# A hybrid layer kernel: the expert tiles' down product in three passes, one tile later

## The reference

```
x = x + mamba2(norm(x))        # 128 heads of 64, 8 groups, state 128
x = x + ffn(norm(x))
x = x + masked_linear(norm(x)) # 512 x 512, 32 x 32 blocks masked
x = x + ffn(norm(x))           # the same weights again
```

```
gu_s = x2 @ shared_w_gate_up.T ; g_s, u_s = split(gu_s)
shared_out = silu(g_s) * u_s @ shared_w_down.T
probs = softmax(x2 @ gate_w.T)
topk_vals, topk_idx = top_k(probs, 2)      # of 16 experts
topk_vals = topk_vals / sum(topk_vals)
g, u = split(einsum('th,eih->eti', x2, w_gate_up))   # 128 + 128 per expert
out_e = einsum('eti,ehi->eth', silu(g) * u, w_down)  # 128 -> 512
ffn = einsum('eth,te->th', out_e, combine) + shared_out
```

## Time and profile before

| what | us |
|---|---|
| median of 3 runs | 2001.85 |
| the profiled execution's own time | 1995.66 |
| its span, first to last instruction | 1993.9 |
| TensorE busy | 1960.6 |
| first tile loop, from the first tile's products | about 1656 to 1753.5 |
| second tile loop | about 1859 to 1957 |

### The profile page before, as it was taken

The page is one execution under the profiler, slowest core; times in us unless marked ns, Lnnn a source line. Parts: engine busy times, 40 slices in busy tenths (PEclk is TensorE's granted clock), DMA queues, the critical chain, the costliest instruction groups (busy, mean ns, idle before and its releaser), DMA issues.

```text
span 1993.9 us, 38125 instructions
## 1 busy us (share of the span) xinstructions
PE 1960.6 (98%) x11776; PEld 1632.7 (82%) x11776; DVE 1467.4 (74%) x2764; ACT 1191.9 (60%) x2602; POOL 1032.7 (52%) x907
## 2 busy tenths in 40 slices
PE   5999999999999999999999999999999999999999
PEld 4888888888888888888888888888888878877887
DVE  8998499849975997599759966996698673167315
ACT  4795388538853884388448744974496444534442
POOL 1596059616951694179417932792289315440433
PEclk8999999999999999999999999999999999999999
DMA  3552145114511351234123413341243139951996
GB/s 107 168 168 58 42 121 168 57 40 124 163 53 57 120 155 48 73 111 152 44 88 109 140 44 93 113 131 43 92 130 113 54 107 327 378 156 48 313 386 198
DMA packets 143909, 253.92 MB, mean 127 GB/s; under 512 B 21448, under 2 KB 37832, under 8 KB 143696
## 3 DMA queue, kind: packets, MB, share of 16 engines
q1 hardware_dynamic: 134848, 231.35, 36.8%
q0 software_dynamic: 7520, 16.80, 2.8%
q10 hardware_dynamic: 1328, 3.15, 0.4%
HBM read 233.38 MB, written 25.69 MB: 130 GB/s over the span
## 4 chain that ended last, share of the span: by engine, by line
PE 91%; DVE 5%; issue 2%; ACT 1%; DMA 1%; DVEq 0%; ACTq 0%; SPq 0%; POOL 0%; POOLq 0%
PE bank L1683 61%; PE bank L1802 7%; PE bank L1992 6%; PE bank L1816 6%; PE bank L1756 4%; PE bank L2004 3%; PE bank L1784 2%; DVE Y L1283 1%; PE bank L1979 1%; PE bank L1691 1%; DVE spare L1380 1%; PE bank L1775 1%; PE bank L1823 1%; DVE Y L1292 1%; DMA cv<-xn_dram,toks 0%
## 5 line engine op out<-in xcount | busy, mean ns | idle before, releaser
L1683 PE MATMUL bank<-xh,wh 128*128 128x512 f32 x1288 | 523.9, 407 | 7.4 <-POOL wl L720 4.0
L1683 PE MATMUL bank<-xh,wl 128*128 128x512 f32 x1288 | 504.9, 392 | 0.0
L1683 PE MATMUL bank<-xl,wh 128*128 128x512 f32 x1288 | 502.8, 390 | 0.0
L720 POOL TENSOR_TENSOR wl<-raw,wh 128x512 fp32r<-128x512 f32 x144 | 192.8, 1344 | 456.7 <-ACT wh L870 456.7
L1283 DVE SCALAR_TENSOR_TENSOR Y<-bank,cpar,Y 128x511 f32<-128x511 f32 (+2 forms) x384 | 286.8, 747 | 23.3 <-ACT Y L914 13.9
L1683 PEld LDWEIGHTS bank<-xh,wh 128*128 128x128 f32 x1288 | 243.0, 189 | 57.2 <-POOL wl L720 4.9
L1683 PEld LDWEIGHTS bank<-xh,wl 128*128 128x128 f32 x1288 | 242.3, 188 | 54.4
L1683 PEld LDWEIGHTS bank<-xl,wh 128*128 128x128 f32 x1288 | 243.4, 189 | 45.8 <-issue 0.5
L737 POOL TENSOR_TENSOR Y<-Y,gt 128x512 f32<-128x512 f32 x128 | 184.1, 1439 | 94.5 <-DVE gt L1337 92.7
L1345 DVE TENSOR_TENSOR al<-Y,ah 128x512 fp32r<-128x512 f32 x128 | 95.8, 749 | 184.3 <-ACT ah L972 184.3
L1683 PE MATMUL bank<-wh,ah 128*128 128x512 f32 x544 | 213.6, 393 | 0.5
(11 more groups left out here) (231 smaller groups left out, 4028.2 us busy)
## 6 DMA issues: line engine op xcount, KB each, us to landing
mem<-c_rows SPq DMA_DIRECT2D x128, 256.0 KB, 3.9
mem<-wffn_d SPq DMA_DIRECT2D x62, 512.0 KB, 6.2
E<-e_rows SPq DMA_DIRECT2D x256, 96.0 KB, 3.5
raw<-wconv_d SPq DMA_DIRECT2D x80, 256.0 KB, 3.0
cv<-c_rows SPq DMA_DIRECT2D x64, 256.0 KB, 4.0
spare<-c_rows SPq DMA_DIRECT2D x64, 256.0 KB, 4.1
raw<-wgate_d SPq DMA_DIRECT2D x64, 256.0 KB, 2.7
raw<-wout_d SPq DMA_DIRECT2D x64, 256.0 KB, 2.7
```

Of the source, the lines that this page charges most:

```text
L720: inc(pool.tensor_tensor(wl[:, W_SLOT[p], :], raw[:, R_SLOT[p], :], wh[:, W_SLOT[p], :], ALU.subtract), w_lo)
L1683: got = mm(out, l, r, start=first and n == 0, stop=last and n == 2)
```

## The change

The hidden rows and the expert's down weights are each split into a high and a low part, and the down product becomes three passes. ACT makes both high parts (`t_hid_hi`, `t_down_hi`), VectorE both low parts. They lie in free places of `ah`, `al`, `wh` and `wl`, two buffers for the weights and four for the hidden rows. TensorE's down product moves from iteration k+1 of a tile to k+2, and with it the output and the store; the loops of TensorE, ACT and SP have one iteration more. The buffers of the down weights and of the hidden rows are released by VectorE's subtraction (`td_lo`, `th_lo`) and no longer by TensorE's product (`ty_mm`). The first high part of the second shared half's hidden rows waits for all down products, since it uses the same memory. The four semaphores `fraw_in` are merged with `raw_in`.

```diff
@@ SP
             def tile_down(run, tau):
                 if tau >= DN_RING:
-                    sp.wait_ge(ty_mm, job(run, tau - DN_RING) + 1)
+                    sp.wait_ge(td_lo, job(run, tau - DN_RING) + 1)
                 elif run:
-                    sp.wait_ge(ty_mm, TILES)
+                    sp.wait_ge(td_lo, TILES)
...
-                for k in range(TILES + 1):
+                for k in range(TILES + 2):
...
-                    if k:
-                        tile_out(run, k - 1)
+                    if k >= 2:
+                        tile_out(run, k - 2)
@@ ACT
+                if i % 2:
+                    act.wait_ge(ty_mm, job(i // 2, TILES))
...
                 if tau >= H_RING:
-                    act.wait_ge(ty_mm, job(run, tau - H_RING) + 1)
+                    act.wait_ge(th_lo, job(run, tau - H_RING) + 1)
...
+            def t_down_hi(run, tau):
+                act.wait_ge(td_in[tau % DN_RING], 16 * uses(DN_RING, run, tau))
+                if tau < 2:
+                    now(act, dn_mm, 2 * run, TT)
+                else:
+                    act.wait_ge(ty_mm, job(run, tau - 2) + 1)
+                nc.scalar.activation(down_rows(tau, 0), tdn[tau % DN_RING], ACT.Copy).then_inc(td_hi, 1)
+
+            def t_hid_hi(run, tau):
+                act.wait_ge(tg_h, job(run, tau) + 1)
+                if tau >= 4:
+                    act.wait_ge(ty_mm, job(run, tau - 4) + 1)
+                nc.scalar.activation(hid_rows(tau, 0), thid[tau % H_RING], ACT.Copy).then_inc(th_hi, 1)
...
                     if 0 <= k < TILES:
                         t_tanh(run, k)
+                        t_hid_hi(run, k)
                     if k + 2 < TILES:
                         t_rows_evac(run, k + 2)
-                    if 0 <= k - 1:
-                        t_out(run, k - 1)
+                    if 0 <= k - 1 < TILES:
+                        t_down_hi(run, k - 1)
+                    if 0 <= k - 2:
+                        t_out(run, k - 2)
@@ VectorE, at the end of t_hidden, and behind it
+                    dve.wait_ge(th_hi, n)
+                    TTn(hid_rows(tau, 1), hid, hid_rows(tau, 0), ALU.subtract).then_inc(th_lo, 1)
+
+                def t_down_lo(tau):
+                    dve.wait_ge(td_hi, job(run, tau) + 1)
+                    TTn(down_rows(tau, 1), tdn[tau % DN_RING], down_rows(tau, 0), ALU.subtract).then_inc(td_lo, 1)
...
                 for tau in range(TILES):
                     t_hidden(tau)
+                    if tau:
+                        t_down_lo(tau - 1)
+                    if tau == TILES - 1:
+                        t_down_lo(tau)
@@ TensorE
                 def t_down(tau):
-                    pe.wait_ge(tg_h, job(run, tau) + 1)
-                    pe.wait_ge(td_in[tau % DN_RING], 16 * uses(DN_RING, run, tau))
+                    pe.wait_ge(th_lo, job(run, tau) + 1)
+                    pe.wait_ge(td_lo, job(run, tau) + 1)
...
-                    mm(bank[YB[tau % 2]][:, :], thid[tau % H_RING], tdn[tau % DN_RING], start=True,
-                       stop=True).then_inc(ty_mm, 1)
+                    three(bank[YB[tau % 2]][:, :], hid_rows(tau, 0), hid_rows(tau, 1), down_rows(tau, 0),
+                          down_rows(tau, 1), True, True, True).then_inc(ty_mm, 1)
...
-                for k in range(TILES + 1):
+                for k in range(TILES + 2):
...
-                    if k:
-                        t_down(k - 1)
+                    if k >= 2:
+                        t_down(k - 2)
```

More of the change, by code:

```diff
@@ L287, in hybrid_layer @@
         dn_acc = counted("dn_acc", TT)
-        fraw_in = [sem(f"fraw_in{n}") for n in range(NRAW)]
         sp_in, spm_in, rt_in = sem("sp_in"), sem("spm_in"), sem("rt_in")
@@ L306, in hybrid_layer @@
         tx_mm, tx_ok = sem("tx_mm"), sem("tx_ok")
+        td_hi, td_lo, th_hi, th_lo = sem("td_hi"), sem("td_lo"), sem("th_hi"), sem("th_lo")
         tg_mm, tg_th, tg_hg, tg_h = sem("tg_mm"), sem("tg_th"), sem("tg_hg"), sem("tg_h")
@@ L468, in hidden_rows, with down_rows, hid_rows @@
             return (wl if low else wh)[:, s, :].rearrange("p (a b) -> p a b", a=4)
+        def down_rows(tau, low):
+            return (al if low else ah)[:, tau % 2, :, :].rearrange("p a b -> p (a b)")
+        def hid_rows(tau, low):
+            return (wl if low else wh)[:, 10, tau % 4 * P:(tau % 4 + 1) * P]
         def job(run, tau):
@@ L563, in shared_in @@
                 sp.dma_start(raw[:, p % NRAW, :], wffn_d[3 * (EXPERTS + 2 * (i % 2)) + p]).then_inc(
-                    fraw_in[p % NRAW], 16)
+                    raw_in[p % NRAW], 16)
             experts = wffn_d[0:3 * EXPERTS].rearrange("(e k) p n -> e p k n", k=3)
@@ L630, in fraw_arrived @@
         def fraw_arrived(eng, i, p):
-            eng.wait_ge(fraw_in[p % NRAW], 16 * (i * (2 if p % NRAW < 2 else 1) + (2 if p >= NRAW else 1)))
+            mixer = GROUPS * R_COUNT[p % NRAW]
+            eng.wait_ge(raw_in[p % NRAW], 16 * (mixer + i * (2 if p % NRAW < 2 else 1) + (2 if p >= NRAW else 1)))
         @block.gpsimd
@@ L1119, in _ @@
                 hidden_hi(first, 3)
-                for k in range(-2, TILES + 1):
+                for k in range(-2, TILES + 2):
                     if 0 <= k < TILES:
                         t_tanh(run, k)
+                        t_hid_hi(run, k)
                     if k + 2 < TILES:
                         t_rows_evac(run, k + 2)
-                    if 0 <= k - 1:
-                        t_out(run, k - 1)
+                    if 0 <= k - 1 < TILES:
+                        t_down_hi(run, k - 1)
+                    if 0 <= k - 2:
+                        t_out(run, k - 2)
                     if 1 <= k <= 4:
```

## The result

The change made the kernel slower: 2013.79 us, median of 5 runs (2011.96 to 2017.07), against 2003.16 (2001.73 to 2006.36) for the kernel before on the same chip. The ratio, in brackets its 95% interval, is 1.0058 [1.0046, 1.007], 11.6 us of loss (the two medians differ by 10.6) where I had forecast 3.2 of gain. 2013.79 lies above my range, which ended at 2008.5.

The account below looks back on a forecast made before the run. TensorE, busy 98% of the span, was taken as the bound, with DMA nearly full beside it. Beats near 3.05 us made 93.95 us per run, 3.2 us gained in all: 1998.7 us forecast, range 1992 to 2008.5.

Parts of the forecast that it names:

- VectorE's two splits: VectorE, tile loops: 128x128 low part hidden behind ACT's copies; 128x512 takes 0.69 to 0.75 us, fits by under 0.2 us.
- TensorE's passes: Down product in the tile loops: three passes cost 0.68 us instead of 0.86, saving 0.15 a tile; TensorE's beat becomes 2.94.
- ACT's two splits: ACT's high-part copies in the tile loops: next tanh possible at 2.59 us, so hidden; 3.10 where ACT copies another weight.
- DMA: Middle of the tile loops: bytes stay, nearly full transfer engines, not TensorE, set the new beat at 3.05 us.
- Rival C: SP's wait on VectorE's split ahead of the down load starves loads: beat 3.25 us, 2007.9 us in all; chance 0.24.
- I price it at nothing: SP's later down, gate and up loads in the tile loops: ring depth hides the delay, so no cost was counted.
- SP is at 3.1 already: Argument for starved loads: SP's own work per tile in the loops, 2.75 to 3.14 us, is already near its limit.
- Rival D: ACT-VectorE semaphore hand-offs set the loop beat at 3.1 us: 2.3 us over the forecast, 2001.0 us; chance 0.11.
- Ends of the loop: Behind each loop's last tanh: two down products move to the end, the last product ending 4.24 us after that tanh.
- The sum: Each feed-forward run, first tanh to last down product's end: 93.95 us; gains of 1.3 and 1.9, together 3.2 us.

Follow-up runs that it names:

- all cures: Changed kernel plus GpSimd's loop arithmetic moved to VectorE and spread out, four down-weight buffers, each loop's last tile one f32 matmul: 2001.35 us, 0.9973 of kernel before.

## Why the prediction was wrong

*The step that failed* is "VectorE's two splits": the 128x512 one "takes 0.69 to 0.75", and the 128x128 one "is hidden behind ACT's copies". Both prices hold only while GpSimd does no arithmetic beside them; where it did, they were up to 4.11 and 2.10 us. The rows that I took the price from the earlier trace rows were of other stages; in the tile loop VectorE's steps had PSUM as one input, the `bank` in the earlier trace rows, and so there was nothing to meet. I had listed GpSimd's queue only for its gathers. Undoing the meeting gives back 0.36 of the 0.58%, and moving the work rather than leaving it out gives back 0.33, the same within the intervals. Against the 93.95 us that my sum has for each run, from the first tanh to the end of the last down product, the profile has 103.7 and 98.5.

The price in the earlier trace rows already had the meeting in it. Of the 128 subtractions whose mean I read as 749 ns the median is 693, but eight, one in each group of the mixer, took 1.57 us, beside a GpSimd instruction with its inputs in SBUF:

```profile
189.14 1.30 POOL L737 TENSOR_TENSOR Y<-Y,gt 128x512 f32<-128x512 f32 x1 [0.20 <-DVE gt L1337]
...
189.41 1.57 DVE L1345 TENSOR_TENSOR al<-Y,ah 128x512 fp32r<-128x512 f32 x1 [0.35 <-ACT ah L972]
```

A mean of 749 above a median of 693 was the sign in the trace of before.

The Trainium skill, "SBUF — State Buffer", section "Who interferes with whom", says that VectorE shares one pair of SBUF ports with GpSimd, as an exclusive lock: an instruction of VectorE with two inputs in SBUF contends with one of GpSimd that reads SBUF, and with at most one such input, outside the modes that use two ports, it does not. By that rule the new subtractions collide and the old steps don't; the traces agree (904 and 558 ns beside GpSimd's arithmetic, 692 and 294 without). It is the rule that spoke against this change, and I had not weighed it.

*TensorE's passes*: right. Free beats are 2.91 to 2.94, forecast 2.94.

*ACT's two splits*: 3.16 where it copies another weight, forecast 3.10; but followed by one of 2.68 (that tile is let through late and the next catches up), so that a single such tile and the next took 5.84 together, where 3.10 and 2.94 make 6.04.

*DMA*: in the second loop some middle beats were 3.2 to 3.3 in the changed kernel, above my 3.05, and others 2.92. With half of the down weights all were 2.92, but with the fourth buffer alone so were they at full bytes, so a steady beat set by the engines is not borne out. In the first loop the term never came to bear, 340 GB/s.

*Rival C*, SP's queue: the runs speak for its mechanism, since a deeper ring with earlier loads was worth 0.21% with the port free, and the delay alone costs 0.2% in the kernel before. If so, "I price it at nothing" was wrong by some 4 us. But C wasn't what made the changed kernel slow: alone, the deeper ring changed 0.02%, with intervals that would hide 0.2 but not 0.58. "SP is at 3.1 already" was a misreading: the 3.14 were the loop's own beat, and in the changed kernel SP's down loads leave 2.91 to 2.97 us apart where nothing is held (1725.04, 1727.95, 1730.87, 1733.84).

*Rival D*: not borne out. With 20 more instructions on VectorE the two loops together got no longer than with GpSimd's work left out (182.6 us both times), and with the fourth buffer alone twelve iterations in a row had TensorE's beat of 2.91 to 2.94, hand-offs included.

*Ends of the loop*: the length was right, t+4.24 forecast and 4.37 measured in the first run. Left out were the clock after the idle 1.95 us (5.03 in the second), and that the last stores and with them the gathers start 3.7 us later behind the last tanh; by the waits shown above, VectorE passes part of that on to the masked product. Curing TensorE's part gave 0.17% twice, by two different edits.

*The sum*: by the steps from 1.0058 over 1.0025 and 1.0008 to 0.9987 the port has 0.33% (0.36 with the work left out), the ends 0.17 and the ring 0.21, 0.71% in all, of which 0.13 lie below the kernel before. That they add up to the measured loss proves nothing, since the steps are taken one from the other. What stands by itself is the port, with its control, and the ends, which gave 0.17 by two edits. The ring's share is read across two chips and is the least certain.

*Open*: with all cures, from the last tanh of the first loop to the first of the second it takes 115.9 us, in the first trace of before 109.9. The waits at the masked product (1.81 and 0.81 us) and 1.56 us for VectorE ahead of it are part of that, and a clock of 0.88 to 0.95 over 20 us; whether the kernel before is as slow there on that chip is not known, since no profile of it was taken there. What the late gathers cost by themselves wasn't tried either, nor what ACT's new wait for all down products, ahead of the second shared half, costs.

## What to carry to other kernels

When a change gives VectorE an instruction with both inputs in SBUF, look at what GpSimd runs at that time, not at how busy VectorE is: a subtraction of 0.69 us took up to 4.1. And take the price of an instruction from its shortest, median and longest, not from its mean: here the longest showed the meeting before the change was made. Arithmetic that GpSimd does for nothing may be better done by VectorE itself once VectorE has such instructions, in half the time here. And before delaying a product by a tile, count what the last tile then drags behind the loop, through its store and gathers as well as on TensorE, and leave that tile in the old form if need be.

## What the runs showed of the hardware

- VectorE's held instruction can start before GpSimd's record does: L1582 began at 1736.19, 0.65 us before GpSimd's (1736.84), and would have ended at 1736.48; it was held all the same. GpSimd's gathers did not hold it: L1582 at 1687.07 took 0.29 us within a gather of 1686.94 to 1687.94.
- An idle time of 1.95 us on TensorE was followed by a granted clock of 0.50 in some places and not in others: in the changed kernel behind the second loop but not the first, in the profile of the same kernel on the third chip behind both, in the kernel with four buffers alone (the same 1.95) behind neither. With GpSimd's instructions shrunk, it fell after 1.76 us behind the first loop (0.61 and 0.54 in the 4 us after the idle time), and after the 1.17 and 1.18 us of the reordered end it did not fall. This is the stretch behind the second loop with four buffers alone, where 0.50 stood in the changed kernel:

```profile
1970.00:1972.00 2.00, 2.00 (x9) 1.66 (x10) 0.00 (x0) 1.12 (x2) 0.00 (x0) 1.00 0.39 147
```

- The same 128x512 subtraction takes 1283 ns on GpSimd and 685 on VectorE.
